# One buffer of gathered rows, gathered a block later, in a conditioned residual kernel of four layers

## What is computed

```
def L0(x, mu, W_dec, b_dec, V):            # per entry a decoded low-rank weight
    U = (mu @ W_dec + b_dec).reshape(B, 257, 30)
    param = einsum('bik,kj->bij', U, V)
    return einsum('bsd,bde->bse', x, param[:, :-1]) + param[:, -1][:, None]

def L1(x, w, weight, bias, aw, ab):        # modulated and demodulated product
    styles = w @ (aw / sqrt(128)).T + ab
    d = rsqrt(sum((weight[None] * styles[:, None]) ** 2, axis=2) + 1e-8)
    return clip(einsum('blc,oc->blo', x * styles[:, None], weight) * d[:, None] + bias, -256, 256)

def L2(x, cond, ...):                      # adapter with weights made per entry
    act = relu(einsum('bsd,bdh->bsh', x, down_p * dg[:, None] + db[:, None]))
    return einsum('bsh,bhd->bsd', act, up_p * ug[:, None] + ub[:, None]) + x

def L3(x, pathway_ids, compartment_ids, time_steps, scale_type, ...):
    h = ln(x, pw_g[pathway_ids], pw_b[pathway_ids])      # rows gathered by token
    h = ln(h, cp_g[compartment_ids], cp_b[compartment_ids])
    t = ln(x, tm_g[time_steps], tm_b[time_steps])
    m, n, r = (x + mlp_ln(state)[:, None] for state in (memory, noise, resource))
    s = ln(x, ms_g[scale_type], ms_b[scale_type])
    cat = concatenate([w0*h, w1*t, w2*m, w3*n, w4*r, w5*s], -1)
    return mlp_ln(cat)                                   # silu(cat @ W1 + b1) @ W2 + b2, then ln

x = x + L0(x); x = x + L1(x); x = x + L2(x); x = x + L3(x)
```

## Time and profile before

| | |
|---|---|
| three runs, median (lowest to highest) | 524.81 us (524.8 to 526.4) |
| the profiled execution, its own time | 520.52 us |
| its span, first to last instruction | 518.7 us |
| mean granted clock of TensorE | 0.981 of 2.4 GHz |
| busy: TensorE, VectorE, ScalarE, GpSimd | 482.6, 409.4, 355.6, 410.7 us |
| four indirect DMAs per chunk, all | 64 issues, 63.9 us, 0.998 us each on average |
| bytes moved | 61.81 MB, 119 GB/s on average |

### The profile page before, as it was taken

The page is one execution under the profiler, slowest core; times in us unless marked ns, Lnnn a source line. Parts: engine busy times, 40 slices in busy tenths (PEclk is TensorE's granted clock), DMA queues, the critical chain, the costliest instruction groups (busy, mean ns, idle before and its releaser), DMA issues.

```text
span 518.7 us, 9591 instructions
## 1 busy us (share of the span) xinstructions
PE 482.6 (93%) x3190; PEld 359.1 (69%) x3219; DVE 409.4 (79%) x701; ACT 355.6 (69%) x671; POOL 410.7 (79%) x383
## 2 busy tenths in 40 slices
...
GB/s 302 259 347 155 150 116 82 0 175 111 168 35 173 1 244 4 223 25 206 42 187 61 162 86 120 128 79 169 59 190 52 198 36 87 50 11 154 41 1 81
DMA packets 35021, 61.81 MB, mean 119 GB/s; under 512 B 5017, under 2 KB 17445, under 8 KB 34612
## 3 DMA queue, kind: packets, MB, share of 16 engines
...
HBM read 52.61 MB, written 8.87 MB: 119 GB/s over the span
## 4 chain that ended last, share of the span: by engine, by line
PE 72%; POOL 8%; DVE 6%; DMA 5%; issue 4%; ACT 3%; SPq 0%; DVEq 0%; POOLq 0%; ACTq 0%
PE ps_d L973 10%; PE ps_c L923 10%; PE ps_c L925 10%; PE ps_c L924 10%; PE ps_d L987 5%; PE ps_a L1001 4%; PE ps_b L923 3%; PE ps_b L924 3%; PE ps_b L925 3%; DMA ugub<-ugub_scratch 3%; PE ps_b L1019 3%; POOL pw_rows L1537 2%; PE ps_a L1013 2%; PE ps_a L1019 2%; DMA set_wdec<-in_W_dec 1%
## 5 line engine op out<-in xcount | busy, mean ns | idle before, releaser
L1537 POOL DMA_INDIRECT pw_rows<-in_pw,gidx x64 | 63.9, 998 | 18.4 <-issue 17.7
L973 PE MATMUL ps_d<-xm_t,l_w 128*128 128x512 f32 x128 | 58.8, 602 | 4.0 <-DVE h L1458 2.3
L1239 ACT ACTIVATE h<-h,nb_h,rstd_h 128x256 f32<-128x256 f32 x64 | 33.2, 591 | 34.8 <-POOL nb_h L1567 34.6
L1546 POOL TENSOR_TENSOR xm_t<-x_t,style 128x1024 f32<-128x1024 f32 x16 | 30.5, 1905 | 19.8 <-DVE x_t L1375 19.7
L973 PEld LDWEIGHTS ps_d<-xm_t,l_w 128*128 128x128 f32 x128 | 23.1, 190 | 28.8 <-issue 24.6
L1582 POOL TENSOR_TENSOR h<-xhat,pw_rows 128x1024 f32<-128x1024 f32 x16 | 38.0, 2373 | 4.7 <-ACT xhat L1239 4.1
L1601 POOL TENSOR_TENSOR w_up<-up_rep,ugub 128x1024 f32<-128x1024 f32 x16 | 38.2, 2385 | 2.7 <-issue 1.3
L1603 POOL TENSOR_TENSOR w_up<-w_up,ugub 128x1024 f32<-128x1024 f32 x16 | 39.0, 2436 | 1.3
L1587 POOL TENSOR_TENSOR h<-h,pw_rows 128x1024 f32<-128x1024 f32 x16 | 38.3, 2391 | 1.2
L923 PE MATMUL ps_b<-w_h,act_t_l 128*128 128x256 f32 x128 | 37.7, 295 | 0.4 <-DVE act_t_l L1480 0.4
L1613 POOL TENSOR_TENSOR x3be<-x,ln_gb 128x1024 f32<-128x1024 f32 x16 | 37.9, 2366 | 0.0
...
## 6 DMA issues: line engine op xcount, KB each, us to landing
...
pw_rows<-in_pw,gidx POOLq DMA_INDIRECT x64, 3.7
...
```

Source lines behind the costliest of these rows:

```text
L973: m = eng.matmul(ps_l1[:, o, :], l1_w[:, k, o * P:(o + 1) * P], xm_t[:, k, :], start=k == 0, stop=k == KB - 1)
L1239: m = eng.activation(out[:, j, :], src[:, j, :], ACT.Identity, bias=nb[k][:, j:j + 1], scale=rstd[k][:, j:j + 1])
L1537: eng.indirect_dma_start(pw_rows[c.ring][:, j, :], None, t["pw"], bass.IndirectOffsetOnAxis(ap=gidx[c.ring][:, j:j + 1], axis=0)).then_inc ...
```

## The change

Five things are changed.

- `pw_rows` is one buffer instead of two, in a place of its own. `g_gather` of chunk n now waits for the add of chunk n-1, the last reader of the buffer, instead of chunk n-2.
- The gather has lag 3 in the loop instead of 2, in the same slot. So one gather fewer stands in `begin` and one more in `end`, where each of the three stands directly behind an add; the gather of chunk 1 does so too, that of chunk 2 keeps its place behind `w_up` of chunk 2.
- The gather of chunk 0 stands ahead of `g_b2rows` and no longer waits for `pe_hid`; the weights `w1_mem` and `w1_nr` lie in `y_sq`, which is not used until the end of chunk 0.
- Outside of the loop the gathers take their indices from `pw_idx` directly, and the copies into `gidx` for them are gone (5 of 16).
- `g_b2rows` still splits the bias into three pieces, but no longer selects them by six small operations on masks; three DMAs from GpSimd's queue write the rows of `b2_row`. Who waits for `g_b2` waits for 48 instead of 2.

```diff
+        pw_rows = sb("pw_rows", [P, CT, 2 * D])
...
+        w1_mem, w1_nr = (y_sq[:, 2 * i:2 * i + 2, :].rearrange("p a d -> p (a d)").bitcast(F32) for i in range(2))
...
-        late("gap", [P, 13 * 32])
-        pw_rows = [late(f"pw_rows{r}", [P, CT, 2 * D]) for r in (1, 0)][::-1]
...
         def g_b2rows(eng, c):
-            eng.wait_ge(d_id, 16)
             eng.wait_ge(v_w2c, 1)
             pieces = [p[:, :] for p in b2p]
             split(eng, g_link, b2f[0][:, :], b2f[1][:, :], b2f[2][:, :], *pieces)
-            g_link(eng.tensor_scalar(b2f[1][:, :], pieces[0], ident[0:PIECES, 0:1], None, ALU.mult))
-            for e in range(1, PIECES):
-                g_link(eng.tensor_scalar(b2f[2][:, :], pieces[e], ident[0:PIECES, e:e + 1], None, ALU.mult))
-                if e < PIECES - 1:
-                    g_link(eng.tensor_tensor(b2f[1][:, :], b2f[1][:, :], b2f[2][:, :], ALU.add))
-            for u in range(CH // D):
-                eng.tensor_tensor(b2_row[0:PIECES, u * D:(u + 1) * D], b2f[1][:, :], b2f[2][:, :],
-                                  ALU.add).then_inc(g_b2, 1)
+            for e in range(PIECES):
+                eng.dma_start(b2_row[e:e + 1, :].rearrange("p (u d) -> p u d", d=D),
+                              pieces[e][e:e + 1, :].unsqueeze(1).broadcast_to([1, CH // D, D])).then_inc(g_b2, 16)
...
         def g_gather(eng, c):
 
             if first(c):
-                eng.wait_ge(m_hid, 1)
                 eng.wait_ge(d_late, 48)
-            wait(eng, g_h1, c.n - 1)
-            wait(eng, s_pw[c.ring], 16 * CT * c.half)
-            if isinstance(c.n, int) and c.n == 1:
-                eng.wait_ge(g_dc, 1)
-                eng.wait_ge(m_dc, 1)
-                eng.wait_ge(d_ug, 16)
-            wait(eng, a_gidx, c.n + 1)
+            wait(eng, g_h1, c.n)
+            if isinstance(c.n, int):
+                idx = pw_idx[:, c.n * CT:(c.n + 1) * CT]
+            else:
+                wait(eng, a_gidx, c.n - 2)
+                idx = gidx[c.ring][:, :]
             settle(eng, s_idle)
             for j in range(CT):
-                eng.indirect_dma_start(pw_rows[c.ring][:, j, :], None, t["pw"],
-                                       bass.IndirectOffsetOnAxis(ap=gidx[c.ring][:, j:j + 1], axis=0)).then_inc(s_pw[c.ring], 16)
+                eng.indirect_dma_start(pw_rows[:, j, :], None, t["pw"],
+                                       bass.IndirectOffsetOnAxis(ap=idx[:, j:j + 1], axis=0)).then_inc(s_pw[c.ring], 16)
...
-                      order=[(g_wup, 3), (g_hmul, 4), (g_hadd, 4), (g_tlow, 2), (g_rooty, 6), (g_gather, 2),
+                      order=[(g_wup, 3), (g_hmul, 4), (g_hadd, 4), (g_tlow, 2), (g_rooty, 6), (g_gather, 3),
```

More of the change, by code:

```diff
@@ L1149, in pe_w2 @@
             if first(c):
-                eng.wait_ge(g_b2, 2)
+                eng.wait_ge(g_b2, 16 * PIECES)
                 eng.wait_ge(g_w2l, 1)
@@ L1328, in act_gidx @@
         def act_gidx(eng, c):
-            if first(c):
+            if isinstance(c.n, int):
                 eng.wait_ge(d_late, 48)
@@ L1581, in g_hmul @@
             wait(eng, p_hht, c.n)
-            eng.tensor_tensor(h1[:, :, :], xhat[:, :, :], pw_rows[c.ring][:, :, 0:D], ALU.mult).then_inc(g_h1m, 1)
+            eng.tensor_tensor(h1[:, :, :], xhat[:, :, :], pw_rows[:, :, 0:D], ALU.mult).then_inc(g_h1m, 1)
         def g_hadd(eng, c):
             eng.wait_ge(g_h1m, c.n + 1)
-            eng.tensor_tensor(h1[:, :, :], h1[:, :, :], pw_rows[c.ring][:, :, D:2 * D], ALU.add).then_inc(g_h1, 1)
+            eng.tensor_tensor(h1[:, :, :], h1[:, :, :], pw_rows[:, :, D:2 * D], ALU.add).then_inc(g_h1, 1)
         def g_rooth(eng, c):
@@ L1699, in _ @@
                              (act_hh, 1), (act_th2, 4), (act_x3h, 2), (act_tmh, 1), (act_ysquare, 0),
-                             (act_relu, 3), (act_msh, 1), (act_xht, 2), (act_gidx, 4)],
-                      order=[(act_u, 1), (act_hnorm, 4), (act_silu, 5), (act_gidx, 1), (act_silh, 5),
+                             (act_relu, 3), (act_msh, 1), (act_xht, 2)],
+                      order=[(act_u, 1), (act_hnorm, 4), (act_silu, 5), (act_gidx, 2), (act_silh, 5),
                              (act_th1, 1), (act_x3, 3), (act_xnorm, 3), (act_hh, 4), (act_th2, 1), (act_tmh, 4),
@@ L1704, in _ @@
                              (act_x3h, 3)],
-                      end=[(act_hnorm, 12), (act_u, 15), (act_gidx, 15), (act_silu, 11), (act_silh, 11),
+                      end=[(act_hnorm, 12), (act_u, 15), (act_silu, 11), (act_silh, 11),
                            (act_th1, 15), (act_x3, 13), (act_xnorm, 13), (act_hh, 12), (act_tmh, 12),
@@ L1760, in _ @@
             run_slots(eng,
-                      begin=[(g_ones, 0), (g_init, 0), (g_b2rows, 0), (g_gather, 0), (g_tlow, 0), (g_style, 0),
+                      begin=[(g_ones, 0), (g_init, 0), (g_gather, 0), (g_b2rows, 0), (g_tlow, 0), (g_style, 0),
                              (g_dcoef, 0), (g_wup, 0), (g_w1tlow, 0), (g_tlow, 1), (g_moroot, 0), (g_w1xlow, 0),
-                             (g_gather, 1), (g_style, 1), (g_rootx, 0), (g_wup, 1), (g_hmul, 0), (g_hadd, 0),
+                             (g_style, 1), (g_rootx, 0), (g_wup, 1), (g_hmul, 0), (g_hadd, 0), (g_gather, 1),
```

29 lines of the change are left out of this document (14 added, 15 removed).

## The result

The changed kernel takes 533.15 us in the median (531.54 to 535.61), the kernel before 524.81: ratio 1.0155, interval 1.0104 to 1.0207. Run again beside more runs of before it was 532.79 against 525.65, ratio 1.0135 (1.0110 to 1.0161). It is slower by 7 to 8 us. The forecast was 529.1, range 525.3 to 532.0: the direction holds, the size does not. The profiled execution took 534.63 us, its span is 532.8.

What follows compares the result with a forecast made beforehand. TensorE was taken as the bound on the whole, hiding GpSimd in the body, but not in setup, entry and end. Setup -2.6, entry +1.9 and end +5.0 gave +4.3 us on the 524.81 median: 529.1, range 525.3 to 532.0.

Steps and rivals of the forecast that it cites:

- setup (to l1 1): Setup, 17 to 63 us: earlier gather 0 lets t_st 0 and ugub come earlier, gain 2.6 us, bounds 0 and 3.1.
- entry (l1 1 to 4): Entry, 63 to 144 us: moved gather 1 delays l1 2 by 3.6 us; l1 4 comes 1.9 us late.
- body: Loop body: gathers only change places and TensorE hides GpSimd, price nothing.
- end, to l1 15: End: gathers 13 and 14 behind the adds delay the roots of y, so l1 15 is 1.45 us late.
- end, from l1 15: End: gather 15 ahead of w_up 15 makes TensorE stand still for 3.6 us.
- rival D: The new gap at the end: granted clock falls to half, 1.7 us more, 530.8 us; chance 0.06.
- Gather 13: End: behind the add of chunk 12 it delays the root of y 10, l1 14 starts 1.3 us later.
- Rival A: Setup: no early gain, the decoder pays for the gather beside it, 531.7 us; chance 0.16.
- The price put on the copies: Setup: two decoder copies on VectorE slowed beside gather issues, 1.2 us, leaving a gain of 1.4.
- The slack I let l1 3 to 4 take up: Entry, step from l1 3 to l1 4: 28.9 against TensorE's 27.2, slack of 1.7 us absorbs part of the delay.
- B: Entry: one gather fewer ahead of the loop counts in full, -5.0 us, 522.2 us, faster; chance 0.10.
- C: End: the stall at w_up 15 is made up, end costs 1.45, 525.6 us; chance 0.12 with its like.

Runs made afterwards that it cites:

- r_after: The changed kernel, unchanged, run again beside more runs of the kernel before: 532.79 us, ratio 1.0135.
- e_warm15: The changed kernel with 18 more matmuls on constants on TensorE ahead of the up product 15: 531.66 us.
- e_setup_only: The kernel before with the new setup alone (gather 0 first, bias rows by DMA): 524.86 us, ratio 0.9988.
- e_style_first: The changed kernel with gather 1 behind x3be 0 and t_st 2, ahead of the root of h 0: 533.41 us.

## Why the prediction was wrong

**The base.** I added my sum to the median as if both kernels shared what set the median apart from the profile. They don't: both later profiles of before are 4.3 to 4.4 us longer than the first, and 3.3 to 3.4 of that are ScalarE's stall at gather 3, which the first profile lacked and which the change takes away by having no gather there. Against the first profile the change costs 532.8-518.7 = 14.1 us, where the sum was 4.3. Against the other two (spans 523.1 and 523.0) it is 9.7 to 9.8. So the sum was 9.8 us too small for the profile that it was made from, and that the time shows a miss of only 4.0 is luck: 4.3 were put onto the base for another reason, and the changed kernel's profile was itself 1.5 above its median.

| term | forecast | against the first profile | against the other two |
|---|---|---|---|
| setup (to l1 1) | -2.6 | +0.3 (r_after -2.6) | -0.4 (means of w_up 0: -1.9) |
| entry (l1 1 to 4) | +1.9 | +4.3 | +0.6 |
| body | 0 | 0.0 | 0.0 |
| end, to l1 15 | +1.45 | +3.4 | +3.4 |
| end, from l1 15 | +3.6 | +6.1 | +6.1 |

With -1.9 for the setup the last column gives 8.2, which is what the medians show (8.3).

**The step that failed most: the end.** "Total +5.0", with 5.7 as the upper bound, is 9.5 (3.4+6.1). Two of its three terms are the mechanisms named and were sized too small; the third, gather 14, works through a wait that I had left out.
- Gather 15 ahead of w_up 15. From l1 15 to up 15 it is 17.21 us before and 21.46 after, +4.25 instead of 3.6. The 0.65 between them are the first issue's wait of 0.82 us, which I took at 0.17. Then comes what I had as rival D, with a chance of 0.06: the granted clock is 0.72 over 472 to 478, right behind the wait. e_warm15 prices it at 1.6, near the 1.7 that D gave.

```profile
472.00:478.00 6.00, 5.02 (x23) 4.63 (x24) 3.05 (x4) 2.08 (x4) 4.57 (x7) 0.72 0.00 0
```

- Gather 13. +1.3 was forecast, +2.04 came; its first issue waited 0.83 us too, which makes up most of the difference. y_out 10 did wait for rstd_y, as foreseen; VectorE's timeline of after, against the earlier trace rows:

```profile
415.05 1.66 DVE L1508 SCALAR_TENSOR_TENSOR y_out<-ps_b,rstd_y,x3be 128x256 f32<-128x256 f32 x4 [2.81 <-POOL rstd_y L1618]
```

- Gather 14. I gave l1 15 only 0.15 more, by way of the root of y. But t_st 15 stands behind this gather too: TensorE waits 2.10 us for it, and xm_t 15 starts 26.67 us behind l1 14 where it was 25.31. That is +1.36.

**Setup: right in kind, 1.9 for 2.6.** t_st 0 came at 33.35 (32.7 foreseen). The gather's megabyte did go into the free DMA (share 0.99 from 20 to 28 us, 0.67 before), yet ugub did not gain as much: with 0.9 MB less to move in all from 28 to 48 us, the queue that carries ugub took 91.1% of the engines' time for 4.80 MB, against 76.3% for 4.65 MB before. The DMA queues of after in that stretch, against the earlier trace rows:

```profile
q1 hardware_dynamic: 3006, 4.80, 91.1%
...
q0 software_dynamic: 96, 0.00, 0.3%
```

So free bandwidth ahead of 28 us was not the limit for all of the gain. What was isn't settled: the three kernels that keep the load of x_t 2 out of that queue have w_up 0 at 44.4 to 45.5, another 1.0 earlier in the mean, but the ranges overlap. Rival A (no gain) is out on the mean, though the changed kernel's own profile looks just like it, and e_setup_only shows no gain in its time.

The price put on the copies, which would have left 1.4 of the gain, did not come. The two copies that started at 17.95 and 21.55 us beside gather issues took 0.65 and 0.62 us, as before. It was the issues beside them that were long: 1.52 us for the first, where r_after, with no copy beside it, has 1.09, and 1.15 for the third. The long copy (1.13 now, 1.22 before) is at 15.7 in both kernels, beside a cast of GpSimd, and there it matters who is first. In before the cast starts at 15.48 and takes 0.81 us, the copy starts at 15.60 and takes 1.22. In r_after the copy starts at 15.47 and takes 0.65, the cast starts at 15.50 and takes 1.31.

**Entry: 4.3 for 1.9.** At l1 2 it is +5.5 for 3.6 forecast. Beside the issue's wait (0.84 for 0.17) there is a leg that I took to be through in time: t_st 2 behind the gather, TensorE's wait of 5.11 us for it, and the clock at half from 84.6 to 91.4 us, in that wait and behind it. e_style_first shows that this leg and the root of h are near level: easing the one shortens the step by 0.9 us only, and the other, with its own wait and half clock, adds 1.7 to the next step. The slack I let l1 3 to 4 take up was 1.2, not 1.7: its floor is 27.6. That the whole entry costs only 0.6 against the two later profiles of before is mostly the stall's doing (3.3 to 3.4).

**Rivals.** B had the right object with the wrong reason: a gather less ahead of the loop does gain 4.5 us in that step (32.1 to 27.6), 3.3 of it by ScalarE's stall and 1.2 by the slack, not 5 by GpSimd's sum; and the move of gather 1 takes it back. C is out. Body at nothing: right to 0.1 us over nine chunks.
